# S4 convolution and quantised FFN on one core: weight loads in 2 KB pieces, one first convolution, later ones in slot 0

## Chip, core and metric

One NeuronCore of a Trainium2 chip runs the whole kernel. The metric is the device time of one execution in microseconds. TensorE (PE) multiplies and transposes, VectorE (DVE) and ScalarE (ACT) work elementwise, GpSimd (POOL) too; SyncE (SP), ScalarE and GpSimd each have a queue from which DMA transfers are issued.

## What is computed

```python
# x (64, 32, 512) f32: batch, head, time; length (64,)
dt = exp(log_dt); A = -exp(log_A_real) + 1j * A_imag          # (32 heads, 64 states)
K = 2 * einsum('hn,hnl->hl', C * (exp(A*dt) - 1) / A, exp((A*dt)[..., None] * arange(512))).real
u = x * mask(length)
y = (causal convolution of u with K over 512 steps + u * D) * mask     # the reference does it by FFT
xq = int4_quant(y)                     # per row: round(y * sqrt(7) / (mean|y| + eps)), clipped to -8..7
# bitlinear: weights become -1, 0, 1: clip(round(w / (mean|w| + eps)), -1, 1), times mean|w|
gate, up = bitlinear(xq, w_gate), bitlinear(xq, w_up)         # 512 -> 1376
inter = int8_quant(up * relu(gate)**2)
out = x + bitlinear(inter, w_down)                            # 1376 -> 512
```

The rounding of a weight matrix needs the mean of all its magnitudes, so it can't begin before the whole matrix is in.

## The kernel before

The 2048 rows (batch x head) are 16 tiles of 128 rows. Tile n holds head n and head n + 16 of all 64 batches. The convolution of a tile is 16 matmuls: the tile, transposed, against Toeplitz rows of the head's kernel K (128 x 512 for each of the two heads), which are read back from a DRAM buffer (`k_back`) with a stride of one element, 512 KB a tile (`load_toep`, L362 to L365).

**Front.** K is built from tables of powers. VectorE makes the parameters, then the power tables of heads 0 to 3 of each half (`raise_powers`, `left_factors`, L986 to L991, semaphore `early_tables`); GpSimd makes those of the other heads in two parts (L474 to L484). `k_sums(i)` on TensorE, `k_copy(i)` on VectorE and `store_k(i)` on SyncE then write K to DRAM, part by part.

Beside it the weights w_gate and w_up (1376 x 512 f32, 2.8 MB each) and the first quad of x (1 MB) are loaded. `load_inner` (L328 to L333) loads a matrix in two parts. The rows are spread as `(p c)`: partition p gets ten consecutive rows, of which part 0 takes six (12 KB in one piece) and part 1 four (8 KB). SyncE issues part 0 of w_gate, part 0 of w_up and half of x; ScalarE part 1 of both and the other half of x. The last 96 rows (the tail, block 10) are loaded by GpSimd's queue (L430). For each part: `weight_sum` (|w| with a running sum, ScalarE), then, when all parts are summed, `mean(m)` on TensorE, `weight_mean(m)` on VectorE (semaphore `winv_ready`), `weight_round` to int16 (ScalarE or VectorE), then twelve `turn`s on TensorE, each of which transposes two blocks of 128 rows into a PSUM bank, and a `weight_copy` for each, which clips to -1..1 and writes `gate_t` or `up_t` (ScalarE or VectorE, by the tables `COPY_ACT` and `COPY_DVE`). TensorE's order is written out by hand (L580 to L607): turns, transposes of x (`xt`), convolutions 0, 1 and 2 and the first `first_q` stand interleaved; `keep_clock` are matmuls whose result nobody reads.

**Slots.** For m in 0..15 (L672 on): `products(m, 0..2)` (gate and up in three chunks of 416, 512 and 448 columns), `xt(m+4)`, the down projections that are due (`DOWNS`, from slot 5 on), and `conv(m+4)`. Slot 0 also holds conv(3) and `first_q(1)`. ScalarE does relu and square of each chunk (L780, L783), the sum (`y_sum`) and rounding (`y_round`) of the tile two slots ahead, and `xt_copy(m+4)`. VectorE multiplies and finds the maximum (L1099, L1103), scales, quantises (`inter_q`, L1144), clips q of tile m+2 (`q_copy`) and masks tile m+4 (`y_mask`). SyncE issues DMA transposes of q and inter_q, Toeplitz loads and stores. VectorE's quantisation in slot m waits until the transpose of inter_q of slot m-1 has landed (L1141).

**w_down.** GpSimd issues its loads behind all its tables (L486 to L492); ScalarE sums it in slots 0 and 1; in slot 2 ScalarE and VectorE round two blocks each (`down_round`), reading with a stride of ten elements to undo the `(p c)` spread; SyncE transposes the four blocks by DMA (`turn_down`) in slots 2 and 3. GpSimd loads x's quads 2 and 3 in slot 2.

All three producers of a slot run in order, so an instruction that waits holds up everything behind it on its engine.

## Time and profile before

| | |
|---|---|
| median of 3 runs | 219.95 us (219.66, 219.95, 222.68) |
| profiled execution | 222.14 us |
| its span, first to last instruction | 220.3 us |
| granted TensorE clock, mean | 0.985 |
| busy: PE, DVE, ACT, POOL | 179.0, 159.1, 116.6, 36.7 us |

All times within the trace count from the span's start. Busy times of PE are those of pipelined matmuls. "Idle before, releaser" says how long an engine stood still and whose event ended it.

### The profile page before, as it was taken

How to read it: one execution, taken by the hardware profiler on the slowest of the kernel's cores; microseconds unless marked ns; L12 is line 12 of the kernel's file. 1: busy time of each engine (PE TensorE's matmuls, PEld its weight loads, DVE VectorE, ACT ScalarE, POOL GpSimd, SP SyncE). 2: the span in 40 equal slices, each digit the busy share in tenths (PEclk: the TensorE clock that was granted, in tenths of full speed). 3: DMA queues.
4: the chain of work that ended last, by engine and by line, in shares of the span. 5: the costliest groups of instructions: out<-in, count | busy, mean ns of one | idle time of the engine just before them, and what ended most of it. 6: DMA issues, size and time to landing. Idle time of an engine off the chain costs nothing.

```text
span 220.3 us, 3351 instructions
## 1 busy us (share of the span) xinstructions
PE 179.0 (81%) x1085; PEld 93.6 (43%) x1085; DVE 159.1 (72%) x424; ACT 116.6 (53%) x189; POOL 36.7 (17%) x88
## 2 busy tenths in 40 slices
PE   1005169969898895975999999999999999999983
PEld 1004066744463442432545454454545444444442
DVE  6996244555677798269986877878796978889662
ACT  2054567448767999044638182644628174450820
POOL 8534923991000052000000000000000000000000
PEclk9999999999999999697999999999999999999999
DMA  5999493728956589999335556473545254471624
GB/s 162 389 323 282 78 299 100 172 95 290 272 139 109 105 197 194 236 295 192 69 119 116 148 110 167 117 159 121 115 119 119 58 101 87 101 148 40 133 51 95
DMA packets 45439, 34.25 MB, mean 156 GB/s; under 512 B 37102, under 2 KB 37390, under 8 KB 44782
## 3 DMA queue, kind: packets, MB, share of 16 engines
q1 hardware_dynamic: 43070, 24.93, 49.2%
q0 software_dynamic: 1760, 6.36, 10.6%
q10 hardware_dynamic: 592, 2.75, 3.8%
q8 instruction: 9, 0.15, 0.3%
q14 instruction: 8, 0.07, 0.1%
HBM read 21.07 MB, written 4.28 MB: 115 GB/s over the span
## 4 chain that ended last, share of the span: by engine, by line
PE 71%; DMA 10%; ACT 9%; issue 5%; DVE 3%; SPq 1%; ACTq 0%
PE gate_ps L619 16%; PE up_ps L624 13%; PE down_ps L656 11%; DMA raw<-in_L_ffn_w_up_dram 10%; PE conv_ps L538 8%; PE tr_dve_ps L538 6%; PE conv_ps L656 4%; PE down_ps L538 3%; PE tr_act_ps L524 3%; ACT g L780 2%; ACT int L723 2%; PE up_ps L562 2%; ACT x_t L737 2%; ACT int L711 1%; PE gate_ps L562 1%
## 5 line engine op out<-in xcount | busy, mean ns | idle before, releaser
L780 ACT ACTIVATE g<-gate_ps,gu_scale 128x416 f32<-128x416 f32 (+2 forms) x48 | 30.5, 635 | 62.2 <-PE gate_ps L619 62.2
L1099 DVE SCALAR_TENSOR_TENSOR inter<-up_ps,gu_scale,g 128x416 f32<-128x416 f32 (+2 forms) x48 | 33.3, 694 | 23.5 <-ACT g L783 21.6
L624 PE MATMUL up_ps<-up_t,q_t 128*128 128x416 bf16 (+2 forms) x192 | 45.0, 357 | 1.8 <-DVE inter L1099 1.8
L619 PE MATMUL gate_ps<-gate_t,q_t 128*128 128x416 bf16 (+2 forms) x192 | 45.2, 358 | 0.1
L1103 DVE TENSOR_REDUCE imax<-inter 128x1 f32<-128x416 f32 (+2 forms) x48 | 30.3, 631 | 1.7
L783 ACT ACTIVATE g<-g 128x416 f32<-128x416 f32 (+2 forms) x48 | 28.1, 586 | 1.5
L656 PE MATMUL down_ps<-down_t,i_t 128*128 128x512 bf16 (+1 forms) x121 | 27.9, 379 | 0.0
L624 PEld LDWEIGHTS up_ps<-up_t,q_t 128*128 128x128 bf16 x192 | 18.6, 98 | 20.7 <-DVE inter L1099 2.7
L619 PEld LDWEIGHTS gate_ps<-gate_t,q_t 128*128 128x128 bf16 x192 | 17.6, 98 | 15.9 <-issue 2.7
L538 PE MATMUL conv_ps<-toep,x_t 128*64 128x512 f32 (+3 forms) x128 | 20.5, 467 | 4.5 <-ACT x_t L737 4.5
L711 ACT ACTIVATE int<-raw 128x2560 bf16<-128x2560 f32 (+2 forms) x6 | 15.2, 2530 | 14.4 <-issue 7.6
L514 PE MATMUL down_ps<-wsum,averaging 128*128 128x1 f32 x12 | 2.5, 314 | 20.8 <-ACT int L711 20.8
L656 PEld LDWEIGHTS down_ps<-down_t,i_t 128*128 128x128 bf16 (+1 forms) x121 | 11.8, 98 | 13.7
L538 PEld LDWEIGHTS conv_ps<-toep,x_t 128*64 128x64 f32 x128 | 9.0, 144 | 17.1 <-issue 9.7
L538 PE MATMUL tr_dve_ps<-toep,x_t 128*64 128x512 f32 (+3 forms) x80 | 13.6, 488 | 2.4 <-ACT x_t L737 2.4
L1144 DVE TENSOR_SCALAR inter_q<-inter,iscale 128x1376 int16<-128x1376 f32 x15 | 14.0, 936 | 0.5
L749 ACT ACTIVATE y_int<-y,yscale 128x512 int16<-128x512 f32 x16 | 11.5, 721 | 3.3 <-DVE yscale L1035 3.2
L514 PEld LDWEIGHTS down_ps<-wsum,averaging 128*128 128x128 f32 x12 | 2.5, 279 | 21.9 <-ACT int L711 21.8
L338 POOL DMA_DIRECT2D raw<-in_x_dram x6 | 5.6, 935 | 37.0 <-DVE winv L982 26.4
L538 PEld LDWEIGHTS tr_dve_ps<-toep,x_t 128*64 128x64 f32 x80 | 5.9, 150 | 11.0 <-issue 7.5
L737 ACT COPY x_t<-tr_act_ps 128x512 f32<-128x512 f32 x16 | 9.1, 571 | 2.1 <-PE tr_act_ps L524 2.1
L656 PE MATMUL conv_ps<-down_t,i_t 128*128 128x512 bf16 (+1 forms) x44 | 10.2, 379 | 0.0
(183 smaller groups left out, 227.4 us busy)
## 6 DMA issues: line engine op xcount, KB each, us to landing
toep<-k_back SPq DMA_DIRECT2D x16, 512.0 KB, 3.9
out_dram<-o_sb SPq DMA_DIRECT2D x30, 128.0 KB, 2.4
raw<-in_x_dram POOLq DMA_DIRECT2D x6, 512.0 KB, 7.8
raw<-in_L_ffn_w_gate_dram SPq DMA_DIRECT2D x1, 1536.0 KB, 14.0
raw<-in_L_ffn_w_up_dram SPq DMA_DIRECT2D x1, 1536.0 KB, 21.7
raw<-in_L_ffn_w_down_dram POOLq DMA_DIRECT2D x1, 1472.0 KB, 10.8
raw<-in_L_ffn_w_down_dram POOLq DMA_DIRECT2D x1, 1280.0 KB, 7.7
raw<-in_L_ffn_w_gate_dram ACTq DMA_DIRECT2D x1, 1024.0 KB, 5.5
```

The lines of the kernel that those rows point to most:

```text
L538: mm = pe.matmul(bank[half * B:(half + 1) * B, 0:L - i * P], x_t[n % 2][:, i, half * B:(half + 1) * B], toep[n % 4][:, half, i * P:L], sta ...
L619: mm = pe.matmul(gate_ps[bank][:, 0:cn], q_t[m % 3][:, i, :], gate_t[:, i, c0:c0 + cn], start=(i == 0), stop=(i == KB - 1))
L624: mm = pe.matmul(up_ps[bank][:, 0:cn], q_t[m % 3][:, i, :], up_t[:, i, c0:c0 + cn], start=(i == 0), stop=(i == KB - 1))
L656: mm = pe.matmul(bank[:], i_t[n % 2][0:r, c, :], down_t[0:r, c, :], start=(c == 0), stop=(c == IB - 1))
L711: nc.scalar.activation(w_bits[m][weight_part(m, i)], raw[m][weight_part(m, i)], ACT.Abs, accum_out=wsum[:, m, i:i + 1]).then_inc(w_summed, 1)
L737: nc.scalar.copy(x_t[n % 2][:].rearrange("p k t -> p (k t)"), tr_act_ps[:]).then_inc(xt_copied, 1)
L749: nc.scalar.activation(y_int[n % 2][:], y[n % 3][:], ACT.Copy, scale=yscale[n % 2][:]).then_inc(y_rounded, 1)
L780: nc.scalar.activation(g2[bank][:, 0:cn], gate_ps[bank][:, 0:cn], ACT.Relu, scale=gu_scale[m % 4][:, 0:1]).then_inc(relu_done, 1)
L783: nc.scalar.activation(g2[bank][:, 0:cn], g2[bank][:, 0:cn], ACT.Square).then_inc(g2_ready, 1)
L1099: v.scalar_tensor_tensor(out=inter[:, c0:c0 + cn], in0=up_ps[bank][:, 0:cn], scalar=gu_scale[m % 4][:, 1:2], in1=g2[bank][:, 0:cn], op0=AL ...
L1103: return v.tensor_reduce(imax[:, c:c + 1], inter[:, c0:c0 + cn], AX.X, ALU.max, apply_absolute_value=True)
L1144: v.tensor_scalar(inter_q[:, 0:I], inter[:], iscale[:], None, ALU.mult).then_inc(inter_quant, 1)
```

## The change

The weights are no longer spread: block c is rows 128c to 128c + 127, row by row on the partitions, so that every piece of a load is one row of 2 KB. Each of w_gate and w_up is loaded in three parts of four, four and three blocks (the third with the tail): ScalarE's queue issues parts 0 and 2 of w_gate, part 1 of w_up and a half of x; SyncE's part 1 of w_gate, parts 0 and 2 of w_up and the other half of x. GpSimd loads no tail. `weight_mean(0)` stands ahead of VectorE's power tables. Six turns stand ahead of conv(0), six behind it, then `first_q(0)`; conv(1), conv(2), conv(3) and xt(3) move into slot 0. `keep_clock(4)` goes. ScalarE's queue issues the loads of w_down ahead of `y_sum(0)`. w_down is rounded without a stride. `q_copy(m+1)` stands behind gated(0) of slot m instead of `q_copy(m+2)` at its end.

```diff
-    SPLIT = 6
+    PARTS = [(0, 4), (4, 8), (8, IB)]
-        TURNS = (0, 1, 6, 7, 2, 8, 3, 9, 4, 10, 5, 11)
-        TURN_BANK = (0, 1, 2, 3, 0, 1, 2, 3, 1, 3, 1, 3)
-        COPY_ACT, COPY_DVE = (2, 3, 4, 8, 10, 11), (0, 1, 5, 6, 7, 9)
+        TURNS = (0, 1, 2, 6, 7, 3, 8, 9, 4, 10, 5, 11)
+        TURN_BANK = (0, 1, 0, 2, 3, 1, 2, 3, 1, 3, 1, 3)
+        COPY_ACT, COPY_DVE = (1, 2, 4, 5, 10), (0, 3, 6, 7, 8, 9, 11)
         def load_inner(eng, m, w, i):
-            full = w[0:WIDE * P, :].rearrange("(p c) k -> p c k", c=WIDE)
-            if i == 0:
-                eng.dma_start(raw[m][:, 0:SPLIT, :], full[:, 0:SPLIT, :]).then_inc(w_loaded[m][0], 16)
-            else:
-                eng.dma_start(raw[m][:, SPLIT:WIDE, :], full[:, SPLIT:, :]).then_inc(w_loaded[m][1], 16)
+            full = w[0:WIDE * P, :].rearrange("(c p) k -> p c k", p=P)
+            c0, c1 = PARTS[i]
+            eng.dma_start(raw[m][:, c0:min(c1, WIDE), :], full[:, c0:min(c1, WIDE), :]).then_inc(w_loaded[m][i], 16)
+            if c1 == IB:
+                eng.dma_start(raw[m][0:IR, WIDE, :], w[WIDE * P:I, :]).then_inc(w_loaded[m][i], 16)
...
-            load_inner(sp, 0, w_gate, 0)
+            load_inner(sp, 0, w_gate, 1)
             load_inner(sp, 1, w_up, 0)
+            load_inner(sp, 1, w_up, 2)
             load_half(sp, 0, 0)
...
-            for m, w in enumerate((w_gate, w_up)):
-                pool.dma_start(raw[m][0:IR, WIDE, :], w[WIDE * P:I, :]).then_inc(tail_loaded[m], 16)
...
 # TensorE
-                if n == EARLY:
-                    pe.wait_ge(q_copied, 2)
+                if n in (2, 3):
+                    pe.wait_ge(q_copied, n - 1)
...
-                pe.wait_ge(xt_copied, EARLY)
-                wait(pe, q_copied, n)
+                pe.wait_ge(xt_copied, n + 2)
...
             mean(0)
+            pe.wait_ge(ident_ready, 1)
+            turn(0)
+            turn(1)
             pe.wait_ge(early_tables, 1)
             k_sums(0)
-            pe.wait_ge(ident_ready, 1)
-            keep_clock(4)
             mean(1)
             xt(0)
-            turn(0)
-            turn(1)
-            xt(1)
             turn(2)
             turn(3)
+            turn(4)
+            xt(1)
+            turn(5)
             keep_clock(2)
             conv(0)
-            turn(4)
-            turn(5)
+            for i in range(6, len(TURNS)):
+                turn(i)
+            first_q(0)
+            k_sums(1)
             xt(2)
-            conv(1)
-            k_sums(1)
-            turn(6)
-            turn(7)
-            turn(8)
-            xt(3)
-            first_q(0)
-            turn(9)
-            conv(2)
-            turn(10)
-            turn(11)
...
                 products(m, 0)
-                if m == 0:
-                    first_q(1)
                 products(m, 1)
                 if m == 0:
-                    conv(3)
+                    conv(1)
+                    conv(2)
+                    first_q(1)
...
-                if m + EARLY < T:
+                if m > 0 and m + EARLY < T:
                     xt(m + EARLY)
                 products(m, 2)
+                if m == 0:
+                    xt(3)
+                    conv(3)
+                    xt(EARLY)
...
 # ScalarE
-            load_inner(act, 0, w_gate, 1)
+            load_inner(act, 0, w_gate, 0)
+            load_inner(act, 0, w_gate, 2)
+            act.wait_ge(dve_consts, 1)
+            nc.scalar.activation(warm[:], averaging[:, 0:1], ACT.Abs)
             load_inner(act, 1, w_up, 1)
             load_half(act, 0, 1)
...
-                nc.scalar.activation(w_int[2][:, k, 0:WIDE * P].rearrange("p (c t) -> p c t", t=P),
-                                     raw[2][:, k, 0:WIDE * P].rearrange("p (t c) -> p c t", c=WIDE), ACT.Copy,
-                                     scale=winv[:, 2:3])
-                nc.scalar.activation(w_int[2][:, k, WIDE * P:I], raw[2][:, k, WIDE * P:I], ACT.Copy,
+                nc.scalar.activation(w_int[2][:, k, 0:I], raw[2][:, k, :], ACT.Copy,
                                      scale=winv[:, 2:3]).then_inc(w_rounded[2][k // 2], 1)
...
-            weight_sum(0, 1)
-            weight_sum(0, 0)
+            for i in range(3):
+                weight_sum(0, i)
             weight_sum(1, 0)
+            weight_round(0, 0)
             weight_sum(1, 1)
+            weight_sum(1, 2)
+            weight_round(0, 1)
             xt_copy(0)
-            weight_round(0, 1)
+            weight_copy(1)
+            weight_copy(2)
+            weight_copy(4)
             xt_copy(1)
-            weight_copy(2)
-            weight_copy(3)
-            weight_copy(4)
+            weight_copy(5)
+            act.wait_ge(w_rounded[0][2], 1)
+            down_rows = w_down.rearrange("(c p) i -> p c i", p=P)
+            for i in range(2):
+                s = weight_part(2, i)
+                act.dma_start(raw[2][s], down_rows[s]).then_inc(w_loaded[2][i], 16)
+            y_sum(0)
+            weight_copy(10)
+            y_round(0)
             xt_copy(2)
-            y_sum(0)
-            weight_copy(8)
-            y_round(0)
-            xt_copy(3)
-            y_sum(1)
-            weight_copy(10)
-            weight_copy(11)
-            y_round(1)
...
                 relu_square(1)
-                if m + 2 < T:
+                if m == 0:
+                    y_sum(1)
+                    y_round(1)
+                    y_sum(2)
+                elif m + 2 < T:
                     y_round(m + 2)
                 relu_square(2)
+                if m == 0:
+                    y_round(2)
+                    xt_copy(3)
...
 # VectorE
+            weight_mean(0)
             scratch_u, scratch_v = inter[:, 0:128], inter[:, 128:256]
...
-            weight_mean(0)
+            weight_copy(0)
             dve.wait_ge(d_loaded, 32)
             k_copy(0)
-            weight_round(0, 0)
             weight_mean(1)
             weight_round(1, 0)
-            weight_copy(0)
-            weight_copy(1)
+            weight_round(0, 2)
+            weight_copy(3)
             weight_round(1, 1)
+            weight_round(1, 2)
...
-            weight_copy(5)
             y_mask(0)
+            weight_copy(6)
+            weight_copy(7)
+            weight_copy(8)
+            y_scale(0)
+            weight_copy(9)
+            weight_copy(11)
+            q_copy(0)
             k_copy(1)
...
                 gated(0)
-                if m == 0:
-                    q_copy(1)
-                if m + 2 < T:
+                if 1 <= m < T - 1:
+                    q_copy(m + 1)
+                if 1 <= m < T - 2:
                     y_scale(m + 2)
...
                 gated(1)
                 if m == 0:
-                    y_mask(3)
+                    y_mask(1)
+                    y_scale(1)
+                    y_mask(2)
+                    q_copy(1)
+                    y_scale(2)
...
-                if m + 2 < T and m + 2 >= 2:
-                    q_copy(m + 2)
+                if m == 0:
+                    y_mask(3)
                 if m + EARLY < T:
                     y_mask(m + EARLY)
```

GpSimd waits for all three parts of w_up to be rounded before it loads quad 1 of x over them. The rounding on VectorE loses its stride in the same way as ScalarE's.

## Rows read from the trace of the kernel before

**Rows 1.** The page's chain that ended last, by line, shares of the span.
```profile
PE gate_ps L619 16%; PE up_ps L624 13%; PE down_ps L656 11%; DMA raw<-in_L_ffn_w_up_dram 10%; PE conv_ps L538 8%; PE tr_dve_ps L538 6%; PE conv_ps L656 4%; PE down_ps L538 3%; PE tr_act_ps L524 3%; ACT g L780 2%; ACT int L723 2%; PE up_ps L562 2%; ACT x_t L737 2%; ACT int L711 1%; PE gate_ps L562 1%
```
**Rows 2.** The same chain in order of time: start, us, what.
```profile
2.59 21.74 DMA raw<-in_L_ffn_w_up_dram
...
35.44 2.31 PE conv_ps L538 x16
...
77.44 2.52 ACT int L723
...
88.20 4.07 PE tr_dve_ps L538 x16
```
**Rows 3.** Windows: us, busy (x) of each engine, PEclk, DMA share, GB/s.
```profile
4.00:6.00 2.00, 0.68 (x5) 0.60 (x5) 1.33 (x8) 0.68 (x2) 2.00 (x5) 1.00 1.01 418
...
14.00:16.00 2.00, 0.00 (x0) 0.00 (x0) 1.83 (x12) 0.76 (x2) 1.69 (x8) 1.00 1.05 279
...
22.00:24.00 2.00, 1.12 (x3) 0.15 (x1) 1.56 (x1) 0.00 (x0) 1.92 (x3) 1.00 0.88 158
...
29.50:31.00 1.50, 1.42 (x7) 1.42 (x8) 0.33 (x3) 0.03 (x1) 0.00 (x0) 1.00 1.04 239
31.00:33.00 2.00, 2.00 (x19) 1.94 (x18) 1.97 (x3) 1.41 (x2) 0.00 (x0) 1.00 1.02 369
```
**Rows 4.** Packets, MB, share of 16 engines: SyncE's queue 30:36, ScalarE's 4:8.
```profile
q1 hardware_dynamic: 721, 1.38, 69.1%
...
q10 hardware_dynamic: 151, 1.11, 66.2%
```
**Rows 5.** DMA issues to landing (the Toeplitz one at 26.26), and SyncE's wait for k's stores.
```profile
raw<-in_L_ffn_w_gate_dram POOLq DMA_DIRECT2D x1, 192.0 KB, 8.8
...
toep<-k_back SPq DMA_DIRECT2D x1, 512.0 KB, 3.8
...
SPq L365 <- DMA k_back<-k_sb: 8.0, 3, 4.0
```
**Rows 6.** Timeline of ScalarE: start, us, operation, idle before.
```profile
24.35 2.76 ACT L711 ACTIVATE int<-raw 128x3072 bf16<-128x3072 f32 x1 [5.31 <-DMA raw<-in_L_ffn_w_up_dram]
...
32.07 2.43 ACT L717 ACTIVATE int<-raw,winv 128x2560 int16<-128x2560 f32 x1
```
**Rows 7.** Timeline of VectorE: first and last of the early tables, roundings, a copy.
```profile
13.90 0.18 DVE L302 TENSOR_TENSOR inter<-pw 128x16 f32<-128x16 f32 x1
...
18.95 0.22 DVE L320 TENSOR_TENSOR ka<-inter 64x64 f32<-64x64 f32 x1
...
31.09 1.82 DVE L996 TENSOR_SCALAR int<-raw,winv 128x3072 int16<-128x3072 f32 x1
...
38.85 0.69 DVE L1002 TENSOR_SCALAR up_t<-up_ps 128x1024 bf16<-128x1024 int16 x1 [3.15 <-PE up_ps L562]
...
76.94 1.39 DVE L1006 TENSOR_SCALAR int<-raw,winv 128x1280 int16<-128x1280 f32 x1
```
**Rows 8.** Timeline of TensorE: mean, k_sums, two turns, first_q, slot 1.
```profile
19.09 1.01 PE L514 MATMUL down_ps<-wsum,averaging 128*128 128x1 f32 x4 [14.30 <-ACT int L711]
20.03 1.27 PE L577 MATMUL tr_dve_ps<-pw,ka 128*40 128x32 f32 x16
...
33.90 1.10 PE L562 MATMUL gate_ps<-ident_bf,int 128*128 128x128 bf16 x16
...
45.82 0.38 PE L548 MATMUL tr_act_ps<-ident_bf,y_int 128*128 128x128 bf16 x4 [1.85 <-ACT x_t L737]
...
60.69 0.88 PE L619 MATMUL gate_ps<-gate_t,q_t 128*128 128x416 bf16 x4
```
**Rows 9.** A window of slot 3 (columns as rows 3), and the page's row of inter_q.
```profile
90.00:92.00 2.00, 2.00 (x12) 0.98 (x8) 0.00 (x0) 0.00 (x0) 0.00 (x0) 0.50 1.04 211
...
L1144 DVE TENSOR_SCALAR inter_q<-inter,iscale 128x1376 int16<-128x1376 f32 x15 | 14.0, 936 | 0.5
```
**Rows 10.** Waits: who waited for whom, us in total, times, longest.
```profile
DVE iscale L1143 <- DMA raw<-inter_q: 6.0, 1, 6.0
```

More of the change, by code:

```diff
@@ L197, in adaln_ffn @@
         rest_loaded = sem("rest_loaded")
-        w_loaded = [[sem(f"w_loaded{m}{i}") for i in range(2)] for m in range(3)]
-        tail_loaded = [sem(f"tail_loaded{m}") for m in range(2)]
+        w_loaded = [[sem(f"w_loaded{m}{i}") for i in range(3)] for m in range(3)]
         x_loaded = [sem(f"x_loaded{q}") for q in range(QUADS)]
@@ L222, in adaln_ffn @@
         winv_ready = sem("winv_ready")
-        w_rounded = [[sem(f"w_rounded{m}{i}") for i in range(2)] for m in range(3)]
+        w_rounded = [[sem(f"w_rounded{m}{i}") for i in range(3)] for m in range(3)]
         w_turned = sem("w_turned")
@@ L481, in _ @@
                 if i == 0:
-                    for j in range(2):
+                    for j in range(3):
                         pool.wait_ge(w_rounded[1][j], 1)
                     load_quad(pool, 1)
-            pool.wait_ge(toep_loaded[0], 32)
-            for i in range(2):
-                pool.wait_ge(w_rounded[0][i], 1)
-            down_rows = w_down.rearrange("(c p) i -> p c i", p=P)
-            for i in range(2):
-                s = weight_part(2, i)
-                pool.dma_start(raw[2][s], down_rows[s]).then_inc(w_loaded[2][i], 16)
             pool.wait_ge(winv_ready, 3)
@@ L508, in mean @@
             def mean(m):
-                pe.wait_ge(w_summed, 2 * m + 2)
+                parts = 2 if m == 2 else 3
+                pe.wait_ge(w_summed, 3 * m + parts)
                 wait(pe, winv_ready, m)
@@ L512, in mean @@
                     pe.wait_ge(y_masked, EARLY + 2)
-                for i in range(2):
+                for i in range(parts):
                     mm = pe.matmul(down_ps[:, m:m + 1], averaging[:], wsum[:, m, i:i + 1],
-                                   start=(i == 0), stop=(i == 1))
+                                   start=(i == 0), stop=(i == parts - 1))
                 mm.then_inc(w_mean_ps, 1)
@@ L553, in turn @@
                 m, g = TURNS[i] // IG, TURNS[i] % IG
-                pe.wait_ge(w_rounded[m][0 if 2 * g + 2 <= SPLIT else 1], 1)
+                pe.wait_ge(w_rounded[m][g // 2], 1)
                 if turned_before(i) is not None:
```

32 lines of the change are left out of this document (8 added, 24 removed).

## Prediction

> **What bounds the kernel now.** I read the page's chain first [rows 1]: in the long run TensorE sets the time (products, down projection and convolutions), but one part in ten is a DMA, the load of w_up. The chain in order of time [rows 2] says where: up to 24.3 us the end waits for SyncE's load of w_up, then ScalarE sums it [rows 6], and from the first convolution (35.4) TensorE is almost never idle until slot 1 begins at 60.7 [rows 8]. Each microsecond by which the first convolution starts earlier, with what follows it unchanged, comes off the end. A second hole is in slots 2 to 4: ScalarE's rounding of w_down (77.4), a convolution of 4.07 us instead of 2.4 (88.2), and a wait of 6.0 us of VectorE for a transpose of inter_q [rows 2, 10].
>
> Before the first convolution the DMA engines are busy throughout, but what they move falls: 418 GB/s at 4 to 6 us, 279 at 14 to 16, 158 at 22 to 24, where only a half of x on 64 partitions is left [rows 3]. Weights and x are 5.64 and 1.05 MB.
>
> **The new front: loads.** Two queues get the same load: 1 MB of w_gate each, then the rest of w_gate (0.72 MB) beside 1 MB of w_up, then the rest of w_up, and x last. Today half of x (0.5 MB) stands on ScalarE's queue and lands before w_up has finished; now all weights are ahead of x. Nothing of the trace loads weights in 2 KB pieces. Nearest: the Toeplitz loads, 2 KB pieces on one of the same queues: 721 packets took 69.1% of 16 engines x 6 us, so 92 ns each, 356 GB/s; the 8 to 12 KB pieces at 4 to 8 us: 151 packets of 7.4 KB in 66.2% of 16 x 4 us, 281 ns, 420 GB/s [rows 4]. Bounds: 420 above; below, the 240 GB/s that the Toeplitz loads had in their worst stretch (239 at 29.5 to 31) [rows 3]. I take 92 ns, the same size of piece. 2752 packets of weights x 92 ns / 16 = 15.8 us from 3.6 us: weights are in at 19.4 us (17.0 by the upper bound, 27 by the lower), against 24.3. w_gate's first two parts (2.1 MB) are in at 9.1, its third, beside as many bytes of w_up, at 13.2. x (both halves at once, so at up to twice 158 GB/s) at about 22.8. The two tails leave GpSimd's queue, where the first took 8.8 us to land [rows 5].
>
> The Trainium skill (DMA: Bandwidth & Descriptors, Why small descriptors are slow) gives a fixed cost of about three cycles to each packet; a 2 KB piece of 64 beats would lose some 4% by it, which as an estimate from the page is 0.6 us over the weights. The trace's 92 ns against 420 GB/s is a loss of 15%, and the sum goes by the trace.
>
> **Sums and the first mean.** ScalarE sums 3072 elements in 2.76 us and rounds 2560 in 2.43 [rows 6], 0.90 to 0.95 ns an element: 1.9 us for a part of 2048, 1.5 for the third. w_gate: 9.1, 11.0, (landing) 13.2 to 14.8. The mean has three parts instead of two: 1.01 us grows to 1.4 [rows 8]; with VectorE's three small operations winv is there at 16.7.
>
> Here the change adds a wait. weight_mean(0) now stands ahead of the power tables, which VectorE reaches at 13.9 [rows 7]: it stops for 2.8 us. Behind it are the tables (13.90 to 19.17, so 5.3 us), hence k_sums, the store of k and all Toeplitz loads, and GpSimd's tables. The early tables are done at 22.0 instead of 19.2. This is path A: k_sums 1.3 us [rows 8], k_copy, store issued at 23.6. SyncE waited 8.0 us for three stores of k, 4.0 for the longest [rows 5], the first, which stood behind x on its queue: so about 2 each else: Toeplitz loads go out at 26.0 (26.26 before), the first lands 3.8 us later [rows 5]: 29.8. So the added wait is nearly all covered by what the store waited for before; if x is late (as before, 25.9), path A is at 30.1.
>
> Path B: ScalarE sums w_up's first part, rounds w_gate's first (18.7), sums the rest of w_up 19.5 to 23.0, rounds w_gate's second part to 24.9. TensorE: turns 0 and 1 at 18.7, k_sums 22.0, mean(1) 23.3 to 24.7, winv 25.1, xt(0). VectorE rounds w_up's first part in 1.25 (1.82 for 3072 [rows 7]): 26.4. Two turns take 1.1 us [rows 8], so turns 2 to 5, xt(1) and keep_clock end at about 29.4. Both paths meet: first convolution at 29.9 us, 5.5 before. Faster loads alone would give little: path A stays near 29.1. If the loads go by the lower bound, path B is at 37.
>
> keep_clock(4) goes, out of a stretch where TensorE waits, so at nothing; what it warmed is a rival.
>
> **From the first convolution to slot 1.** Before: 35.4 to 60.7, 25.3 us. New, from 29.9, convolutions 2.38 each: masked 33.0; VectorE copies turns 6, 7, 8 (0.6 each), scale, 9 and 11: 36.4; ScalarE rounds y at 36.1; first_q and q_copy 36.9; k_sums(1), xt(2); slot 0 begins at 37.6 (earlier by far than before, but with two convolutions still owed). Two products pairs 3.15 us: 40.7; conv 1 and 2: 45.4; first_q(1) waits for mask, sum, scale and rounding of tile 1, which lie beside conv 2: 46.1; last products 47.6; xt(3) 48.1. conv(3) waits for xt_copy(3), behind relu, square and y_round(2) on ScalarE: 49.3 to 51.6. xt(4) stands behind conv(3) and its copy has nothing beside it: 0.6 + 0.6 us, conv(4) 52.8 to 55.1. Slot 1 begins at 55.1: 25.2 us. The rearrangement by itself is worth nothing; the waits inside (1.1 before conv 3, 0.7 before conv 4, 2 us of turns that wait for copies) stand for those of before (1.85 before first_q [rows 8], about one before conv 4).
>
> The w_down loads leave GpSimd's queue, where they stood behind all tables, and go out from ScalarE at about 31, x's second quad at about 32: 3.8 MB beside 1.3 MB of Toeplitz rows. At 356 GB/s they are in by 46; first needed at 51.6 (xt(4)) and 53 (the sum of w_down). ScalarE's issue costs 1 us while it waits for conv(0). The fifth Toeplitz load, issued at about 40, has 12 us. Covered; were the cover gone, a row that only starts when its convolution could would cost its 3.8 us [rows 5].
>
> Slots 1 and 2 repeat themselves: 5.5 us stay.
>
> **w_down in natural order.** Two strided roundings on ScalarE, 2.5 us each in the chain, and the small ones behind become 1376 contiguous elements, 1.35: ScalarE is free 2.7 us earlier. VectorE's go from 1.39 for 1280 elements and a small one behind to the 0.94 of inter_q's same 1376 [rows 7, 9]: at least 0.9 us for two, about 1.2. Slot 3 then runs without its stall and conv(7) at full clock (4.07 against 2.38): slot 4 begins 3.8 us earlier still. But next in line is the wait for the transpose of inter_q, 6.0 us in VectorE [rows 10], whose transposes stand behind those of w_down on SyncE, with two x quads moving as well. Their bytes are the same, and they start earlier only by what VectorE's rounding saves: 0.5 to 1.2 us. I take 0.5: the gain of slot 3 is given back as a longer wait of TensorE in slot 4.
>
> q_copy moved to the next slot behind gated(0): 0.29 us in another place, its q needed only a slot later. Nothing.
>
> **Sum.** 5.5 + 0.5 = 6.0 us: span 220.3 to 214.3, profiled execution 222.1 to 216.1. The median of the runs shown is 219.95, 2.2 below the profiled one; the gain is taken off the median: 214.0 us.
>
> **Rivals.**
> 1. The 2 KB pieces are slow on the way in: 240 GB/s, as in the Toeplitz loads' worst stretch. Weights end at 27, the convolution starts at 37 instead of 35.4; with 0.5 back later, 221.0 us. It turns slower than before where path B passes 35.9, that is where the last weight lands after 25.9: a mean rate under 253 GB/s. For: Toeplitz pieces at 29.5 to 31 moved at 239. Against: at 31 to 33 they moved at 369 [rows 3]. 15%.
> 2. The clock. After TensorE stood still at 86 to 88 us, the granted clock was 0.50 at 90 to 92 and the convolution took 4.07 [rows 2, 9]. Now keep_clock(4) is gone, TensorE is half idle before the first convolution and again between 33 and 37.6. One or two convolutions at 1.2 GHz, 1.7 each: 215.7 to 217.4; take 216.5. Against: a pause of 1.85 us behind the turns cost no clock before [rows 8]. 20%.
> 3. The wait in slot 4 shrinks further, because w_down and x quad 1 are long in and the transposes start with VectorE's second rounding: 3 us off instead of 0.5, 211.5 us. 12%. Against: the queue behind it is as long.
> 4. It does not arrive: some wait of the new front (winv for VectorE, d_tail, the copies between turns) eats half of the gain, 217 us. 8%.
>
> **How the numbers follow.** The forecast has 45%. 214.0 us; its own spread is 212.5 to 216 (first convolution at 29.1 to 31.5). The range of 8 in 10, 211 to 219.5, leaves out the worse half of rival 1 and a better end of rival 3. 2% of 219.95 (about what a measurement can tell) is 215.55: faster holds most of the forecast, rival 3 and a little of rival 2, 0.56; slower needs 224.4, first convolution at 40 or rivals 1 and 2 together, 0.07; within 2% 0.37.
>
> **What would show it.** w_gate's parts in by 9.5 and 13.5 and w_up by 20; VectorE idle 2 to 3 us before the first weight_mean; early tables at 22; first Toeplitz load issued at about 26; first convolution at 29.9 at 2.4 us; slot 0's first product at 37.6; slot 1 at 55.1; no idle time before ScalarE's relu in slot 3, a longer one of TensorE in slot 4, conv(8) at half clock. Wrong would be: w_up in after 22, convolutions of 4 us before slot 1, a wait for a Toeplitz row or x quad in slot 0, or a wait in slot 4 that is gone.

## The result and the profile after

The changed kernel takes 234.55 us (median of 4 runs, 231.11 to 237.08), the kernel before in the same session 220.32 (median). The ratio is 1.051, 95% interval 1.036 to 1.066: all ratios here leave out executions more than 1.5% above the fastest of their kernel, so this one is 231.9 against 220.7 us, and the profiled execution of the changed kernel (236.36 us, span 234.5) is among those left out. The forecast was 214.0 with a range of 211 to 219.5, so the sign was wrong.

The starts of the stages on TensorE, from the two profiles, show in which of them the time went:

| start, us | before | forecast | after | after less before |
|---|---|---|---|---|
| first convolution | 35.4 | 29.9 | 39.3 | +3.9 |
| slot 1 | 60.7 | 55.1 | 65.5 | +4.8 |
| slot 3 | 79.8 | 74.3 | 84.65 | +4.85 |
| slot 4 | 92.2 | 82.9 | 93.6 | +1.4 |
| slot 5 | 105.4 | 99.4 | 119.4 | +13.95 |
| span | 220.3 | 214.3 | 234.5 | +14.2 |

(The forecast column is the prediction's sum laid out by stage.) The table's 14.2 us are some 3 more than the 11.2 between 231.9 and 220.7; which stage they fall in no trace shows. There are two losses and one gain: 4.8 us by slot 1, 3.4 us won back in slot 3, 12.5 us lost in slot 4.

The chain in order of time names both losses (start, us, what), to hold against [rows 2]:

```profile
2.58 22.62 DMA raw<-in_L_ffn_w_up_dram
...
27.23 1.89 ACT int L703
29.12 3.37 ACT int L697 x4
...
39.35 2.33 PE conv_ps L529 x16
...
84.28 11.91 SPq L382
96.24 12.59 DMA raw<-inter_q
114.90 4.53 PE conv_ps L529 x16
```

w_up still opens the chain, and its load takes 22.6 us instead of getting shorter. New is the stretch from 84 to 109 us, in which no engine works for the end at all: SyncE's queue (SPq) is occupied for 11.9 us by line 382, the DMA transposes of w_down, and then the transpose of inter_q takes 12.6.

The windows of the loads (columns as [rows 3]):

```profile
8.00:10.00 2.00, 0.00 (x0) 0.00 (x0) 1.83 (x16) 1.33 (x2) 0.00 (x0) 1.00 0.76 231
10.00:12.00 2.00, 0.00 (x0) 0.00 (x0) 2.00 (x19) 0.00 (x0) 0.00 (x0) 1.00 0.74 243
...
14.00:16.00 2.00, 0.00 (x0) 0.00 (x0) 0.79 (x7) 0.59 (x1) 1.13 (x6) 1.00 1.03 389
...
18.00:20.00 2.00, 1.07 (x5) 1.07 (x6) 0.00 (x0) 0.88 (x2) 0.00 (x0) 1.00 1.00 192
```

Three kinds of stretch stand here: where all is well, 2 KB pieces move at 389 GB/s, more than the 356 of the forecast. At 8 to 12 us the rate is 231 to 243 with a DMA share of 0.75: the DMA engines are partly idle although megabytes are queued. From 18 to 26 us it is 186 to 251 with a share of 1.0 or more: they are busy and move little. The question of the experiments on the front is what these two are.

What a queue got of the engines, 4 to 8 us (packets, MB, share of 16 engines):

```profile
q10 hardware_dynamic: 567, 1.13, 77.2%
q1 hardware_dynamic: 186, 0.38, 25.8%
```

Both queues hold loads of 2 KB pieces, and in these 4 us ScalarE's (q10) is served three times as often as SyncE's (q1). From 8 us on they are served alike (243 and 241 packets at 8 to 12, 342 and 345 at 12 to 16), so SyncE's queue stays behind by what it lost at the start. The loads show it, size and time to landing:

```profile
raw<-in_L_ffn_w_gate_dram ACTq DMA_DIRECT2D x1, 1024.0 KB, 5.6
raw<-in_L_ffn_w_gate_dram SPq DMA_DIRECT2D x1, 1024.0 KB, 13.3
raw<-in_L_ffn_w_up_dram SPq DMA_DIRECT2D x1, 1024.0 KB, 22.6
...
int<-int SPq DMA_TRANSPOSE x4, 14.7
```

The last row is for slots 3 to 5: the median transpose of w_down lands after 14.7 us; before, the same view had 8.3.

The waits in slot 4, against [rows 10]:

```profile
DVE iscale L1135 <- DMA raw<-inter_q: 16.3, 1, 16.3
PE up_ps L606 <- DVE inter L1087: 10.4, 1, 10.4
```

VectorE waits 16.3 us instead of 6.0 for the transpose, and TensorE 10.4 for VectorE. What is on the queues then, GpSimd's issues first, SyncE's below (start, us, operation, idle before):

```profile
81.72 1.99 POOL L336 DMA_DIRECT2D raw<-in_x_dram  x2 [28.57 <-DVE winv L974]
85.52 1.72 POOL L336 DMA_DIRECT2D raw<-in_x_dram  x2 [1.80 <-ACT int L709]
```

```profile
82.75 13.45 SPq L382 DMA_TRANSPOSE int<-int  x2
96.24 10.60 SPq L394 DMA_TRANSPOSE raw<-inter_q  x1
```

x quads 2 and 3, 1 MB each, go out 3.8 us apart, around the time of the first two transposes of w_down. Issuing those then holds SyncE for 13.45 us, and the transpose of inter_q stands behind them. The windows in the middle of it, the last column above all:

```profile
88.00:90.00 2.00, 1.91 (x12) 0.90 (x10) 1.93 (x7) 1.66 (x3) 0.00 (x0) 1.00 1.40 114
90.00:92.00 2.00, 0.68 (x4) 0.34 (x6) 1.42 (x3) 1.24 (x3) 0.00 (x0) 1.00 1.26 65
...
104.00:106.00 2.00, 0.00 (x0) 0.00 (x0) 0.00 (x0) 0.00 (x0) 0.00 (x0) 0.50 1.29 89
```

DMA share above 1 and 65 to 114 GB/s: transposes and x quads together are the slowest traffic of the kernel. TensorE stands still, the granted clock falls to 0.50 (1.2 GHz), and conv(8) takes 4.53 us (3.92 in the kernel before, which also waits there).

### The profile page after: what moved, and what is told of

Read it like the earlier page. It is cut to its first block, busy times and chain, and to the rows that moved or that the text cites. A ratio compares the mean times of both kernels' runs of the same rounds, so it can differ in the third digit from the quotient of the medians.

```text
span 234.5 us, 3341 instructions
## 1 busy us (share of the span) xinstructions
PE 179.5 (77%) x1069; PEld 95.2 (41%) x1085; DVE 157.3 (67%) x424; ACT 116.2 (50%) x191; POOL 31.9 (14%) x84
## 4 chain that ended last, share of the span: by engine, by line
PE 61%; DMA 15%; DVE 6%; SPq 6%; ACT 6%; issue 4%; DVEq 0%; ACTq 0%
PE gate_ps L601 14%; PE up_ps L606 12%; PE down_ps L638 10%; DMA raw<-in_L_ffn_w_up_dram 10%; PE conv_ps L529 7%; DMA raw<-inter_q 5%; SPq L382 5%; PE conv_ps L638 4%; PE tr_dve_ps L529 4%; PE down_ps L529 3%; PE tr_act_ps L515 3%; ACT int L697 2%; ACT g L764 1%; DVE inter L1087 1%; PE gate_ps L650 1%
## 5 line engine op out<-in xcount | busy, mean ns | idle before, releaser
L606 PE MATMUL up_ps<-up_t,q_t 128*128 128x416 bf16 (+2 forms) x191 | 45.5, 361 | 10.4 <-DVE inter L1087 10.4
L1087 DVE SCALAR_TENSOR_TENSOR inter<-up_ps,gu_scale,g 128x416 f32<-128x416 f32 (+2 forms) x48 | 33.3, 693 | 24.6 <-ACT g L767 24.4
L601 PE MATMUL gate_ps<-gate_t,q_t 128*128 128x416 bf16 (+2 forms) x180 | 43.6, 362 | 0.6
L606 PEld LDWEIGHTS up_ps<-up_t,q_t 128*128 128x128 bf16 x192 | 18.8, 98 | 29.7 <-DVE inter L1087 11.2
L529 PE MATMUL conv_ps<-toep,x_t 128*64 128x512 f32 (+3 forms) x128 | 21.1, 477 | 3.6 <-ACT x_t L720 3.6
L697 ACT ACTIVATE int<-raw 128x2048 bf16<-128x2048 f32 (+3 forms) x8 | 15.6, 1944 | 15.0 <-DMA raw<-in_L_ffn_w_gate_dram 8.7
L732 ACT ACTIVATE y_int<-y,yscale 128x512 int16<-128x512 f32 x16 | 11.5, 720 | 17.7 <-DVE yscale L1025 16.3
L638 PEld LDWEIGHTS down_ps<-down_t,i_t 128*128 128x128 bf16 (+1 forms) x121 | 11.8, 98 | 13.7
L529 PEld LDWEIGHTS conv_ps<-toep,x_t 128*64 128x64 f32 x128 | 9.2, 147 | 16.7 <-issue 10.2
L1135 DVE RECIPROCAL iscale<-gam 128x1 f32<-128x1 f32 x15 | 2.4, 163 | 16.7 <-DMA raw<-inter_q 16.3
L505 PE MATMUL down_ps<-wsum,averaging 128*128 128x1 f32 x16 | 3.4, 324 | 13.3 <-ACT int L697 13.3
L529 PE MATMUL tr_dve_ps<-toep,x_t 128*64 128x512 f32 (+3 forms) x80 | 11.9, 439 | 1.4 <-ACT x_t L720 1.4
L724 ACT ACTIVATE y_abs<-y 128x512 bf16<-128x512 f32 x16 | 9.8, 616 | 5.2 <-DVE y L1017 5.2
L552 PE MATMUL up_ps<-ident_bf,int 128*128 128x128 bf16 (+1 forms) x44 | 4.5, 267 | 8.9 <-ACT int L703 8.9
L638 PE MATMUL conv_ps<-down_t,i_t 128*128 128x512 bf16 (+1 forms) x44 | 10.2, 379 | 0.0
## 6 DMA issues: line engine op xcount, KB each, us to landing
raw<-in_x_dram POOLq DMA_DIRECT2D x6, 512.0 KB, 14.2
raw<-in_L_ffn_w_gate_dram SPq DMA_DIRECT2D x1, 1024.0 KB, 13.3
raw<-in_L_ffn_w_up_dram SPq DMA_DIRECT2D x1, 1024.0 KB, 22.6
```

The lines of the kernel that those rows point to most:

```text
L529: mm = pe.matmul(bank[half * B:(half + 1) * B, 0:L - i * P], x_t[n % 2][:, i, half * B:(half + 1) * B], toep[n % 4][:, half, i * P:L], sta ...
L601: mm = pe.matmul(gate_ps[bank][:, 0:cn], q_t[m % 3][:, i, :], gate_t[:, i, c0:c0 + cn], start=(i == 0), stop=(i == KB - 1))
L606: mm = pe.matmul(up_ps[bank][:, 0:cn], q_t[m % 3][:, i, :], up_t[:, i, c0:c0 + cn], start=(i == 0), stop=(i == KB - 1))
L638: mm = pe.matmul(bank[:], i_t[n % 2][0:r, c, :], down_t[0:r, c, :], start=(c == 0), stop=(c == IB - 1))
L697: nc.scalar.activation(w_bits[m][weight_part(m, i)], raw[m][weight_part(m, i)], ACT.Abs, accum_out=wsum[:, m, i:i + 1]).then_inc(w_summed, 1)
L732: nc.scalar.activation(y_int[n % 2][:], y[n % 3][:], ACT.Copy, scale=yscale[n % 2][:]).then_inc(y_rounded, 1)
```

## Experiments

Theories after the result. **Q** (quads): the rounding of w_down in natural order is done sooner, so GpSimd's wait on it lets x quad 3 go while quad 2 and the transposes are in flight; that is the loss in slot 4. Rival: natural blocks or the new front change something else there. **P** (pieces): the first loss comes from 2 KB pieces. Rivals: GpSimd's small loads, x's half coming too early, the order of the queues. Run again beside the experiments, the kernel before took 223.5 to 223.8 us (median), so every run is compared by its ratio to it.

### Slot 4: which part does it

**Only the rounding.** The kernel before, w_down rounded in one contiguous pass (the reordering that its spread of rows needs is left out):

```diff
-    activation(w_int[2][:, k, 0:WIDE * P].rearrange("p (c t) -> p c t", t=P),
-               raw[2][:, k, 0:WIDE * P].rearrange("p (t c) -> p c t", c=WIDE), ...)
-    activation(w_int[2][:, k, WIDE * P:I], raw[2][:, k, WIDE * P:I], ...)
+    activation(w_int[2][:, k, 0:I], raw[2][:, k, :], ...)   and the same on VectorE
```

> The kernel before, its rounding of w_down without the stride and the reordering (left out, so only times count). By theory Q x quad 3 is then issued 2 to 3 us earlier and runs beside quad 2 and the transposes: VectorE's wait for the transpose of inter_q grows from 6.0 to 10 us or more, slot 5 begins 4 us later, time 223 to 226 against 220. Rival (my prediction's step: the saved ScalarE time is worth 0.5 us): 219.5.

Measured: 231.38 us, ratio 1.036 [1.028, 1.043]. This one local saving costs some 8 us (231.38 against 223.64). Slot 4 began at 89.5 us, 2.7 earlier than before, slot 5 at 114.7, 9.3 later. GpSimd's issues, SyncE's, and the wait:

```profile
77.53 1.99 POOL L338 DMA_DIRECT2D raw<-in_x_dram  x2 [27.03 <-DVE winv L979]
81.33 1.73 POOL L338 DMA_DIRECT2D raw<-in_x_dram  x2 [1.80 <-ACT int L723]
```

```profile
78.57 16.27 SPq L383 DMA_TRANSPOSE int<-int  x2
```

```profile
DVE iscale L1137 <- DMA raw<-inter_q: 16.5, 1, 16.5
```

Quad 3 comes 1.8 us behind the end of quad 2's issue. In the kernel before the two went out at 76.87 and 83.52; here at 77.53 and 81.33. The strided rounding had kept them 2.9 us further apart. The loss was expected at 3 to 6 us.

**The rounding and the natural blocks** (the old front otherwise):

```diff
-    full = w[0:WIDE * P, :].rearrange("(p c) k -> p c k", c=WIDE)
+    full = w[0:WIDE * P, :].rearrange("(c p) k -> p c k", p=P)
```

> The kernel before with natural blocks: 2 KB pieces in its own two parts, queues and order, and the unstrided rounding. Against b_plain_round it differs in the piece size alone. Theory P: w_up lands at 28 or later instead of 24.3, the first convolution moves from 35.4 to 38 or more, 3 us or more above b_plain_round. Rival U: w_up within 1 us of 24.3 and the time within 1 us of b_plain_round.

Measured: 236.37 us, 1.056 [1.047, 1.065]. Slot 5 at 117.4 and first convolution at 39.3 (36.0 with the rounding alone): 2 KB pieces cost 3.3 us even in the old order of loads, and slot 4 is as slow with them as without.

**Quad 3 alone moved**, in the changed kernel, behind the transpose of slot 2's inter_q:

```diff
+    pool.wait_ge(it_loaded[2], 16)
     load_quad(pool, 3)
```

> The changed kernel, with GpSimd's load of x quad 3 held until the transpose of slot 2's inter_q has landed. Theory Q (the second loss comes from quad 3 moving beside quad 2 and the transposes, since the unstrided rounding releases it 1.8 us behind quad 2 instead of 6.6): the transpose lands within 6 us of its issue, VectorE's wait of 16.3 us falls to 6 or less, and the time falls from about 232 by 8 to 10 us, to 222 to 224. Rival R (quad 2 and the transposes alone are enough for it, or the transposes are slow for another reason): the wait stays above 10 us and the time at 229 to 233. The front is untouched: slot 1 begins at about 65.5 by both.

Measured: 231.18 us, 1.033 [1.023, 1.043]. SyncE's queue, and where quad 3 went out:

```profile
83.64 8.88 SPq L382 DMA_TRANSPOSE int<-int  x2
92.56 5.82 SPq L394 DMA_TRANSPOSE raw<-inter_q  x1
...
100.36 4.98 SPq L382 DMA_TRANSPOSE int<-int  x2
105.39 8.31 SPq L394 DMA_TRANSPOSE raw<-inter_q  x1
```

```profile
100.91 1.41 POOL L336 DMA_DIRECT2D raw<-in_x_dram  x2 [16.30 <-DMA raw<-inter_q]
```

The issue of the first two shrinks from 13.45 to 8.88 us, VectorE's wait from 16.3 to 6.9, slot 4 from 25.7 to 16.0. But the new place is on the next pair of transposes: slot 5 now takes 16.8 us, where the kernel with both quads moved (below) takes 10.3. Half a cure: from a ratio of 1.051 to 1.033 is some 4 us, where 8 to 10 were expected. What must be apart is any quad from any transpose of w_down.

**Both quads moved off the transposes**: quad 2 right behind w_down's loads, quad 3 behind the last transpose of w_down. In the kernel before, in it with the contiguous rounding, and in the changed kernel:

```diff
-    pool.wait_ge(winv_ready, 3)
     load_quad(pool, 2)
     ...
+    for k in range(KB):
+        pool.wait_ge(down_turned[k], 16)
     load_quad(pool, 3)
```

> The kernel before (strided rounding as it was), with x quads 2 and 3 taken away from the transposes of w_down: quad 2 goes out right behind w_down's loads, quad 3 once all four blocks of w_down are turned. Theory Q' (x loads on GpSimd's queue and DMA transposes in flight together slow each other, however they are ordered): VectorE's wait of 6.0 us for the transpose of inter_q is gone, the blocks of w_down turn in 4 us each instead of 8 to 11, slot 4 takes about 8 instead of 13.3 us, and the time falls by 4 to 6 us, 215 to 217 where the kernel before has 220. Rival (the transposes are slow by themselves, four of w_down in front of inter_q's): the wait stays at 4 us or more, the time within 1.5 us of before.

> The same with the unstrided rounding (its reordering left out, so only times count). By Q' slot 3 loses its stall on ScalarE as my prediction said, 8.6 us instead of 12.4, and slot 4 has no wait: 8 to 10 us below before, 210 to 212. This is what the unstrided rounding is worth once the quads are out of the way: 3.5 us better than b_quads. Rival: the rounding's start of the transposes, not the quad, made b_plain_round slow; then it stays above 225.

> The changed kernel with the quads moved in the same way (quad 2 behind GpSimd's tables, beside w_down on ScalarE's queue). By Q' all of the second loss goes: slot 1 begins at about 65.5 as in the changed kernel, slots 3 and 4 take 9 and 8 us, and the time is 4.5 us above b_plain_quads, about 215. Rival (something else in slots 3 and 4 of the changed kernel, such as the place of q_copy): above 222.

Measured: 220.29 us, 0.993 [0.987, 0.998], in the kernel before; 218.21, 0.981 [0.970, 0.993], with the contiguous rounding; 218.60, 0.985 [0.977, 0.994], in the changed kernel. The row that decides, of the kernel before with quads moved, and SyncE's queue of the changed kernel with quads moved:

```profile
int<-int SPq DMA_TRANSPOSE x4, 4.4
```

```profile
81.84 3.89 SPq L382 DMA_TRANSPOSE int<-int  x2
85.78 1.61 SPq L394 DMA_TRANSPOSE raw<-inter_q  x1
```

Alone, a pair of transposes holds SyncE for 3.9 us instead of 13.45, and slot 4 lasts 8.8 us instead of 25.7:

```profile
92.73 0.88 PE L602 MATMUL gate_ps<-gate_t,q_t 128*128 128x416 bf16 x4
101.50 0.88 PE L602 MATMUL gate_ps<-gate_t,q_t 128*128 128x416 bf16 x4
```

Theory Q is shown from both sides: the rounding alone makes the loss, and moving the quads removes VectorE's wait in slot 4 in all three kernels. The kernel before had the same fault in a milder form (landing 8.3 us, wait 6.0).

All three are slower than expected (220.3 instead of 215 to 217, 218.2 instead of 210 to 212, 218.6 instead of 215), in part because the expectations started from 220 us for the kernel before, which took 223.8 beside these runs. For the first two the traces show where more of it went. Quad 2 now goes out at 50.4 us, and the DMA transpose of q for the next tile, issued at 54.7, lands after 10.2 us (6.3 in the kernel before, where only w_down's loads are beside it; 11.8 with the contiguous rounding). VectorE waits for it in slot 1, 0.15 us in the kernel before:

```profile
64.94 0.29 DVE L1046 TENSOR_SCALAR q_t<-q_int 128x512 bf16<-128x512 int16 x1 [4.01 <-DMA q_int<-y_int]
```

Slot 1 takes 11.4 us, and 14.65 with the contiguous rounding (wait 5.67), instead of 10.1. Up to there only quad 2's place differs from the kernel before: it is the same fault with another transpose. In the changed kernel with quads moved VectorE does not wait for q in slot 1.

### The first loss: pieces, small loads, x

**Large pieces in the changed kernel**: the spread of rows of before, pieces of 8 and 4 KB; once with everything else as changed (the reordering of w_down left out), once with quads moved and the strided rounding.

```diff
-    full = w[0:WIDE * P, :].rearrange("(c p) k -> p c k", p=P)
+    full = w[0:WIDE * P, :].rearrange("(p c) k -> p c k", c=WIDE)
```

> The changed kernel with the old spread of the weights over the partitions, so that pieces are 8 KB (parts 0 and 1) and 4 KB (part 2) in the same parts, queues and order; the reordering of w_down that this spread needs is left out, so only times count. Theory P (2 KB pieces are what slows the front): w_up is in by 20 instead of 26, the first convolution starts at 33 to 34 instead of 39.3, time 5 us below the changed kernel. Rival U (the loads share unequally between the two queues and x's halves slow what is beside them, whatever the pieces): w_gate's part on SyncE's queue still lands after 13, w_up after 24, the first convolution after 38, time within 1 us of the changed kernel's.

> The changed order of turns, convolutions and queues with 8 and 4 KB pieces (the old spread, strided rounding) and the quads moved. First convolution at 32.7 and slot 1 at 59.2 as in a_big_pieces, 1.5 us better than before; slots 3 and 4 as in b_quads. Time 1 to 2 us below b_quads, 213 to 216, below both kernels. If the order of slot 0 costs what the earlier convolution gives, it equals b_quads.

Measured: 231.08 us, 1.024 [1.012, 1.035], first convolution at 32.7, slot 1 at 59.2, wait in slot 4 21.8 us; and 216.42, 0.974 [0.963, 0.985], first convolution at 33.1 against 38.4 with 2 KB pieces. So the size of the pieces costs 5.3 to 6.6 us here (38.4 - 33.1 and 39.3 - 32.7). But it does not explain the windows: a rate of 389 GB/s is in reach with 2 KB pieces. The next runs go by the two kinds of slow stretch.

**GpSimd's small loads** (two of 64 lengths, three of one scale for 128 partitions) issued at 16 us, not at 5:

```diff
-    for dst, src in ((len_i[0:B], ...), (len_i[B:P], ...), (scl[:, 0:1], ...), ...):
-        pool.dma_start(dst, src).then_inc(rest_loaded, 16)
     ...
+    (the same five, ahead of)
     pool.wait_ge(early_tables, 1)
```

> a_quads (the changed kernel with the x quads moved, 218.6 us) with GpSimd's five small loads of lengths and scales (4-byte pieces) issued at 16 us instead of 4.6. In a_quads and in a_big_pieces the DMA engines stand partly idle between 8 and 14 us (share 0.61 to 0.85, 204 to 284 GB/s), just when these are under way. Theory S (the small loads hold the engines up): the share is 1.0 and 350 GB/s or more between 8 and 14, w_gate's part on SyncE's queue lands by 12.5 instead of 15.2, first convolution 1 to 2 us earlier, 217. Rival (the gap has another cause, such as the tail or the uneven sharing of the two queues): the share between 8 and 14 stays below 0.9 and the time within 0.5 us of 218.6.

Measured (with quads moved): 216.61 us, 0.971 [0.965, 0.977]; first convolution at 35.2 against 38.4, w_gate's part on SyncE's queue in at 12.7 instead of 15.3. The windows, first with the small loads early, then late:

```profile
8.00:10.00 2.00, 0.00 (x0) 0.00 (x0) 1.97 (x21) 1.30 (x2) 0.00 (x0) 1.00 0.82 242
10.00:12.00 2.00, 0.00 (x0) 0.00 (x0) 2.00 (x19) 0.00 (x0) 0.00 (x0) 1.00 0.71 231
```

```profile
8.00:10.00 2.00, 0.00 (x0) 0.00 (x0) 1.97 (x21) 1.23 (x2) 0.00 (x0) 1.00 1.02 342
10.00:12.00 2.00, 0.00 (x0) 0.00 (x0) 2.00 (x18) 0.00 (x0) 0.00 (x0) 1.00 1.05 364
```

The hole at 8 to 12 us was these few hundred elements of 4 bytes: 100 and 133 GB/s more, the DMA share at 1 again. How they idle the engines is not shown.

**x behind the weights**: both halves issued by SyncE once w_up is in, its last rows too (22.2 us).

```diff
-    load_half(sp, 0, 0)          (and load_half(act, 0, 1) on ScalarE)
+    sp.wait_ge(w_loaded[1][1], 16)
+    sp.wait_ge(w_loaded[1][2], 32)
+    sp.wait_ge(w_loaded[1][0], 16)
+    load_quad(sp, 0)
```

> a_quads with both halves of x issued by SyncE only when all of w_up is in. From 18 to 26 us all kernels load at 190 to 280 GB/s, once ScalarE's queue has come to its half of x. Theory X (x's halves, on 64 partitions with 64 KB between their pieces in DRAM, slow what is beside them): weights go on at 350 GB/s or more and w_up is in at 22 to 23 instead of 25 to 26; then x alone takes 5 us more, until 28 to 29, so the first convolution gains at most 1 us: 217.5 to 219. Rival (2 KB pieces are slow by themselves late in the front): w_up within 1 us of 26, the first convolution 3 us later, 221.

Measured (with quads moved): 216.14 us, 0.970 [0.963, 0.977]; first convolution at 34.9, w_up's first part in at 20.3 instead of 24.6, and at 18 to 20 us 324 GB/s instead of 213. The late x is cheap (size, and time to landing):

```profile
x_first<-in_x_dram SPq DMA_DIRECT2D x2, 512.0 KB, 5.9
```

So the second slow stretch was x's half on ScalarE's queue: with its start ahead, this queue came to x while w_up's parts still stood on the other, and took the engines from them. The changed kernel at 18 to 20 us, packets, MB and share:

```profile
q10 hardware_dynamic: 57, 0.26, 68.5%
q1 hardware_dynamic: 59, 0.12, 31.5%
```

**One load for each 2 KB block**, rows in natural order, then the same with the old spread (rows 20 KB apart in DRAM, reordering left out):

```diff
+    for c in range(c0, min(c1, WIDE)):
+        eng.dma_start(raw[m][:, c, :], full[:, c, :]).then_inc(w_loaded[m][i], 16)
```

> a_quads with one load for each natural block instead of one for each part: same 2 KB pieces, same addresses, 20 loads instead of 6. It is the partner of q_spread_2k. If the count of loads costs nothing: 218.6 within 1 us; each further issue is 0.45 us on its queue, beside the transfers.

> q_blocks with the old spread (partition p takes ten consecutive rows), one load for each block, so that pieces are 2 KB too but lie 20 KB apart in DRAM; the reordering of w_down is left out, so only times count. Theory P (the size of a piece counts): same as q_blocks within 1 us, first convolution at 38 to 39. Rival N (what counts is that natural blocks read rows that lie side by side in DRAM): it is as quick as the 8 KB pieces, first convolution at 33, 5 us below q_blocks.

Measured: 215.62 us, 0.967 [0.960, 0.975], first convolution at 35.5, and 216.29, 0.972 [0.964, 0.980], at 35.0. Whether a load's pieces lie side by side or 20 KB apart makes no difference. But cutting the loads did, against 38.4: w_gate's part on ScalarE's queue landed at 9.6 instead of 7.3, and at 18 to 20 us 399 GB/s moved instead of 213. At 4 to 8 us the queues were served evenly (584 to 175 packets with one load for each part):

```profile
q1 hardware_dynamic: 402, 0.75, 53.5%
q10 hardware_dynamic: 400, 0.73, 50.7%
```

That ScalarE's queue then came to x later, and that this is what helped, is a reading and was not tried by itself.

**Both**, small loads and x late, with quads moved; then with the first mean behind the power tables again; with large pieces and strided rounding; and the mended front alone in the changed kernel, quads untouched:

```diff
     (on VectorE, for the second)
-    weight_mean(0)
     (power tables)
+    weight_mean(0)
     weight_copy(0)
```

> a_quads with both mendings of the front: small loads at 16 us, x issued by SyncE once w_up is in. Alone they brought the first convolution from 38.4 to 35.2 and 34.9. If they add up it starts at 31.5 to 32.5 and the time is 213; if each only moves the same wait, 34.5 and 216. x's landing is next in line: w_up in at about 18.5, x 6 us later at 25, its transpose at 25 to 26.

> q_both with weight_mean(0) behind VectorE's tables again, as in the kernel before. My prediction held that the wait which the change adds to VectorE is covered by path A's other waits. Then the first convolution and the time stay within 0.5 us of q_both. Rival (the tables, k_sums and the Toeplitz loads are what the front waits for once the loads are quick): the Toeplitz loads go out 2 to 4 us earlier and the time falls by 1 us or more.

> q_both with 8 and 4 KB pieces and the strided rounding of w_down that they need. The pieces were worth 5 us in the first convolution in a_big_quads against a_quads (33.1 against 38.4), the strided rounding costs some 3 us in slot 3 (a stall of ScalarE and a convolution at half clock). If what made 2 KB pieces slow was mostly the sharing of the queues up to x, little of the 5 us is left: first convolution 1 us earlier than q_both, time 2 us above it, 215. If the piece counts by itself: 211 to 213.

> The changed kernel with the mended front alone, x quads 2 and 3 as they were. The front gives 6 us (first convolution at 32 to 33 instead of 39.3), the wait for the transpose of inter_q stays at 12 us or more: 225 to 227 us, still slower than before. If it is below 220, the quads did not matter by themselves.

Measured: 213.64 us, 0.957 [0.950, 0.964] (5 runs, 213.06 to 215.85); 214.42, 0.963 [0.956, 0.970]; 215.90, 0.971 [0.963, 0.980]; 230.06, 1.029 [1.020, 1.038]. First convolutions at 34.3, 33.6, 32.0 and 33.6 us. The first of these is the fastest version of the study, 4.3% under the kernel before.

In time the two gains add: the ratio falls from 0.985 to 0.971 and 0.970 alone, to 0.957 together. The first convolutions of the profiled executions don't show it (3.2 and 3.5 us alone, 4.1 together), but that of both was profiled at 215.85 us, 2.2 above its median; its twin with the late mean, profiled at 213.74, began 4.8 us earlier than with neither. In the trace of both, 335 to 391 GB/s moved from 4 to 18 us, and the last rows of w_up were in at 20.8, but then x was next in line on TensorE's timeline, and the turns behind it were slow:

```profile
28.24 1.12 PE L519 MATMUL tr_act_ps<-ident,x_first 128*128 128x128 f32 x4 [1.07 <-DMA x_first<-in_x_dram]
...
30.00 1.91 PE L556 MATMUL gate_ps<-ident_bf,int 128*128 128x128 bf16 x16
...
34.27 2.38 PE L533 MATMUL conv_ps<-toep,x_t 128*64 128x512 f32 x16
```

The mean behind the tables changes nothing that can be told apart (the intervals overlap): the wait that the change adds for VectorE is covered. Large pieces still begin the first convolution about 2 us earlier, but their strided rounding gives more back: slot 3 took 12.3 us with them (77.5 to 89.8), 9.0 without. The mended front alone brings the changed kernel's slot 1 to 59.9, 0.8 ahead of before, and its slot 4 still takes 23.6 us:

```profile
DVE iscale L1137 <- DMA raw<-inter_q: 14.2, 1, 14.2
```

Both parts are needed, and the slot 4 part is the larger.

## Why the prediction was wrong

Two steps failed. The larger is the 0.5 us at which it put the wait in slot 4; the other is the landing of the weights at 19.4 us.

**The rate of the loads.** "2752 packets of weights x 92 ns / 16 = 15.8 us from 3.6 us: weights are in at 19.4 us". w_up's parts on SyncE's queue landed at 24.9 and 25.2, its last rows at 27.8. The size 92 ns was not the fault (389 GB/s in a good window). The term lacked two others: the small loads on GpSimd's queue, which before had the tails ahead of them and came later (they landed 15.5 to 18 us after issue, now 5.4 to 8.5), and the head start of ScalarE's queue, which brought x in beside w_up. With small loads and x late w_up's large parts were in by 19.3 and its last rows at 20.8, near the forecast. The rule of the Trainium skill used beside it (DMA: Bandwidth & Descriptors, Why small descriptors are slow) came to 0.6 us; in the start of the first convolution the runs show 2.3 us (34.3 against 32.0) with small loads and x late and 5.3 (38.4 against 33.1) without: here the measurement decides. A slip that changes nothing: 1024 packets at 92 ns end at 9.5 us, as the list of signs has it, and not at 9.1.

**Order of landing.** "now all weights are ahead of x": true in each queue, but not across the two. x came in beside w_up. And the forecast took w_up's first part as in long before the last. It stood on the slow queue and landed at 25.2 us. ScalarE's timeline and TensorE's show what hung on it:

```profile
25.23 1.91 ACT L697 ACTIVATE int<-raw 128x2048 bf16<-128x2048 f32 x1 [6.35 <-DMA raw<-in_L_ffn_w_up_dram]
...
27.14 1.99 ACT L703 ACTIVATE int<-raw,winv 128x2048 int16<-128x2048 f32 x1
```

```profile
29.27 1.87 PE L552 MATMUL up_ps<-ident_bf,int 128*128 128x128 bf16 x16 [8.90 <-ACT int L703]
31.07 1.28 PE L567 MATMUL tr_dve_ps<-pw,ka 128*40 128x32 f32 x16
...
39.28 2.38 PE L529 MATMUL conv_ps<-toep,x_t 128*64 128x512 f32 x16
```

The sum of w_up's first part stands ahead of the rounding of w_gate on ScalarE, which turns 0 and 1 wait for, and k_sums stand behind these on TensorE. So paths A and B, taken as two, were one: tables were done at 25.8 (forecast 22.0), but k_sums ran at 31.1, and the Toeplitz loads were issued at 34.2 instead of 26.0. From 28 to 34 us the DMA engines moved at most 12 GB/s. "winv is there at 16.7" was 20.9, for w_gate's part on the slow queue (13.3 us).

**TensorE between.** "Two turns take 1.1 us." They took 1.87 to 1.9 at 29 and 36 us and 1.07 only at 41.6: with the transposes of x beside them (1.09 instead of some 0.6) about 2 us of the 14 from landing to convolution (the first pair's slowness is hidden behind ScalarE's sums, for which mean(1) waits).

**From the first convolution to slot 1.** Forecast 25.2, measured 26.3 (39.3 to 65.5), before 25.3. Right within 1.1 us, with the order of waits largely as written. The rearrangement by itself, forecast at nothing, cost 0.9.

**w_down in natural order.** Right in its own stage: ScalarE's two in 2.77 us, slot 3 in 9.0, no stall. Wrong in the next: "Their bytes are the same, and they start earlier only by what VectorE's rounding saves: 0.5 to 1.2 us. I take 0.5". The bytes were the same and their overlap wasn't. The working said that quads and transposes would be in flight together, and never asked when quad 3, which waits for that very rounding, would be issued. Slot 4 took 25.7 us, 12.5 more than before, where the forecast had 16.5. The wait was named as next in line, but its end was put earlier, not later; rival 3 even took the wait for shorter.

**The rivals.** Rival 1 (slow loads, first convolution at 37) had the place of the first loss and almost its size (39.3), through slow pieces, which was a part of it only. With "0.5 back later" it came to 221. Rival 2 (clock) was no cause: half clock came with the stall of slot 4 and lengthened conv(8) by 2.2 us over full clock, of which the kernel before already had 1.5. The signs "first Toeplitz load issued at about 26" (34.2) and "w_up by 20" (27.8) failed first, as the text had set them.

By the runs, moving the quads takes the ratio from 1.051 to 0.985: all of the loss in slot 4 and the stall that the kernel before had there. Mending the front as well takes it to 0.957.

## What to carry to other kernels

When an edit makes one engine finish sooner, list every DMA that waits for it, and lay those issues beside what is in flight then: a slow step may have been what kept a bulk load and a row of DMA transposes apart. Hold bulk loads back by an explicit wait on the transposes, not by the accident of a rounding, and look for other transposes at the place to which they move. For a front limited by loads, forecast each queue's landing times apart, look for one queue that gets ahead of the other, and keep tiny loads and later data behind what is needed first.
